# Expert outputs added into memory by adding scatters, in a one-core block of a long convolution and a mixture of experts

## The reference, cut to what matters

```
x1 = x + layernorm(s4d_block(layernorm(x)))
u  = layernorm(x1)                                # input of the expert layer, "normalised rows"
z  = layernorm(u) * g + b
w  = the two largest of softmax(z @ rW + rb), each over their sum     # 2 of 8 experts per token
mixed = sum over the two experts e of w[e] * (gelu(z @ W1[e] + b1[e]) @ W2[e] + b2[e])
out = x1 + layernorm(u + mixed)
```

## Time and profile before

| | |
|---|---|
| median of three runs | 616.25 us |
| the profiled execution | 617.41 us, of which the profile's span is 615.5 |
| PE busy | 516.5 us (84%) |
| DVE busy | 462.6 us (75%) |
| ACT busy | 347.2 us (56%) |
| POOL busy | 223.3 us (36%) |
| moved by DMA | 69.59 MB |

### The profile page before, as it was taken

One profiled execution on the slowest core, in us unless ns is written; L12 is line 12 of the kernel. 1 busy time (PEld: TensorE's weight loads), 2 busy tenths in 40 slices (PEclk: granted clock), 3 DMA queues, 4 the chain that ended last, 5 costly groups with the idle time before them and its releaser, 6 DMA issues. The chain is left out here.

```text
span 615.5 us, 12632 instructions
## 1 busy us (share of the span) xinstructions
PE 516.5 (84%) x2927; PEld 428.5 (70%) x2928; DVE 462.6 (75%) x1412; ACT 347.2 (56%) x751; POOL 223.3 (36%) x195
## 2 busy tenths in 40 slices
PE   0379899869979778978999999999999999957850
PEld 0139888759868664444798888888888988945640
DVE  6999787997886963873687787777778777732885
ACT  6982755654855568431555555555555555561584
POOL 0000666237676773662132232232322322332410
PEclk9997999989989979869999999999999999986995
DMA  6206600101111788245622222222222222119923
GB/s 162 114 0 246 233 1 1 69 2 70 43 53 43 275 269 285 98 142 134 184 79 70 68 86 68 68 86 68 68 77 77 69 78 76 60 43 366 351 103 136
DMA packets 37261, 69.59 MB, mean 113 GB/s; under 512 B 7568, under 2 KB 23696, under 8 KB 36720
## 3 DMA queue, kind: packets, MB, share of 16 engines
q1 hardware_dynamic: 30752, 51.48, 25.9%
q0 software_dynamic: 6480, 17.77, 8.1%
HBM read 42.02 MB, written 27.21 MB: 112 GB/s over the span
## 5 line engine op out<-in xcount | busy, mean ns | idle before, releaser
L1157 POOL DMA_INDIRECT y_rows<-y_sb,dst x71 | 74.7, 1052 | 195.9 <-DVE y_sb L1043 138.6
L1349 PE MATMUL psum<-ws,z_hl 128*128 x426 | 117.3, 410 | 2.0 <-DVE z_hl L1020 2.0
L1368 PE MATMUL psum<-ws,h_hl 128*128 x852 | 115.9, 285 | 0.1
L1368 PEld LDWEIGHTS psum<-ws,h_hl 128*128 128x128 f32 x852 | 103.5, 189 | 0.3 <-issue 0.3
L1121 POOL DMA_INDIRECT z_rows<-zn,pos x64 | 73.3, 1146 | 39.8 <-DVE pos L881 23.2
L1349 PEld LDWEIGHTS psum<-ws,z_hl 128*128 128x128 f32 x426 | 75.2, 188 | 17.1 <-issue 3.0
L595 ACT CAST h_hl<-psum 128x512 fp32r<-128x512 f32 x71 | 41.7, 587 | 72.5 <-PE psum L1358 72.4
L1028 DVE TENSOR_TENSOR hb<-psum,b1r 128x512 f32<-128x512 f32 x71 | 49.1, 692 | 35.3 <-issue 33.8
L587 ACT ACTIVATE z_f<-psum,gb 128x128 f32<-128x128 f32 x142 | 57.0, 452 | 16.7 <-PE psum L1336 14.7
L601 ACT ACTIVATE hg<-hb 128x512 f32<-128x512 f32 x71 | 44.9, 632 | 36.1 <-DVE hb L1028 35.8
L1224 PE MATMUL psum<-pm,ft 128*128 128x256 f32 x256 | 60.2, 395 | 0.4 <-DVE tmp L840 0.4
(11 more groups left out here) (207 smaller groups left out, 887.7 us busy)
## 6 DMA issues: line engine op xcount, KB each, us to landing
z_in<-z_rows SPq DMA_DIRECT2D x71, 129.0 KB
w_raw<-in_dram SPq DMA_DIRECT2D x16, 512.0 KB, 5.6
ya<-y_rows SPq DMA_DIRECT2D x16, 512.0 KB, 5.6
xs<-in_dram SPq DMA_DIRECT2D x8, 512.0 KB, 5.7
x_dram<-xs SPq DMA_DIRECT2D x8, 512.0 KB
out_dram<-acc SPq DMA_DIRECT2D x8, 512.0 KB, 2.6
b1r<-in_dram SPq DMA_DIRECT2D x8, 256.0 KB
x1m<-x_dram SPq DMA_DIRECT2D x4, 512.0 KB
```

The costliest lines, as they stand in the source:

```text
L1157: pool.indirect_dma_start(y_rows, bass.IndirectOffsetOnAxis(ap=dst[q][:, 0:1], axis=0), y_sb[q][:, :], None).then_inc(sem(f"y_out{q}"), 16)
L1349: last = TE.matmul(ps_h[q], z_hl[q][:, a, k], w_at(e1, c, k * F, F), start=n == 0, stop=n == 5)
L1368: last = TE.matmul(ps_y[q], h_hl[q][:, a, k], w_at(e2, c, 1024 + k * H, H), start=n == 0, stop=n == 11)
```

## The change

It replaces the two rows for each token in `y_rows` by one, and has the DMA add into it.

- Stage one: SP stores each batch's normalised rows `zn` to `y_rows` (`store_rows`), 8 stores of 512 KB, each behind the store of x1. These stores now stand ahead of expert 4's weights. ACT also waits for `zn_stored` before it overwrites a `zn` buffer. Two stores of 128 rows of filler set the 2 x 128 rows that padding goes to. The root and the two operations on `rsm` that served `base` are gone.
- Ahead of the loop: the weights `wgt` are stored to `w_rows`, and DVE makes a table `order` that says for each tile how far the scatters of the other parity must have landed: to the one two before the previous tile where the expert is the same, to the previous tile where it is not.
- Per tile: DVE writes `row_of` (the token), then `flag`, then `widx` (which weight). POOL gathers 128 weights of 4 bytes into `wt` by `widx`, four tiles ahead of the scatter. ACT multiplies `y_sb` by `wt` into `yw`, behind `hg` in its part. POOL scatters `yw` with addition into `y_rows`. It waits for SP's `released` and for the scatter two tiles before. SP issues a `release` for tile t behind the load of tile t+6.
- Tail: 8 loads `yr` of 512 KB instead of 16, and x1's load of 2 MB stands ahead of the third. No diagonal matrices, no matmul, no `base`, no sum. DVE takes statistics straight from `yr`, with the results in PSUM. POOL adds x1, except for the last half batch, which DVE adds. All is written out without hardware loops.

```diff
-TRASH = 2 * B * T
+TRASH = B * T
@@ SP, stage one
+            def store_rows(lo, hi):
+                for b in range(lo, hi):
+                    sp.wait_ge(sem("x1_ready"), b + 1)
+                    sp.dma_start(x1_dram[:, b], xs[b][:, :, :]).then_inc(sem("x1_stored"), 16)
+                    sp.wait_ge(sem("zn_ready"), b + 1)
+                    sp.dma_start(y_tok[:, b], zn[buf(b)][:, :, 0:H]).then_inc(sem(f"zn_stored{buf(b)}"), 16)
+                sp.wait_ge(sem("x1_stored"), 16 * hi)
+            store_rows(0, 4)
+            load_expert(sp, 5)
+            store_rows(4, 5)
             sp.wait_ge(sem("kf_mm"), 2)
             sp.wait_ge(sem("fwd_mm"), 16)
             load_expert(sp, 4)
...
@@ SP, tile loop
+            def release(t, q):
+                behind = sp.value_load(order[0:1, bass.ds(t, 1)], min_val=16, max_val=16 * TILES)
+                sp.wait_ge(sem(f"y_out{1 - q}"), behind)
+                sp.sem_inc(sem("released"), 1)
...
+            with sp.Fori(3, (TILES - 3) // 2) as j:
                 load_z(j * 2 + 2, 0)
+                release(j * 2 - 4, 0)
                 load_z(j * 2 + 3, 1)
+                release(j * 2 - 3, 1)
@@ SP, tail
             for n in range(B):
...
+                if n == 2:
+                    sp.wait_ge(sem("x1_in"), 64)
                     sp.dma_start(x1m[:, 0:4], x1_dram[:, 0:4]).then_inc(sem("x1_in"), 16)
+                sp.dma_start(yr[:, n], y_tok[:, B - 1 - n]).then_inc(sem(f"y_in{n}"), 16)
@@ ACT, part(i), behind hg
+                t, q = i - 2, par
+                if live(t):
+                    act.wait_ge(sem("y_ready"), t + 1)
+                    gate(act)
+                    act.wait_ge(sem(f"w_in{q}"), (t - q) * 8 + 16)
+                    m = slot(t, u, -2)
+                    if not early(t, 3):
+                        act.wait_ge(sem(f"y_out{1 - q}"), (t - 2 + q) * 8)
+                    nc.scalar.activation(yw[m % 3][:, :], y_sb[q][:, :], ACT.Identity, scale=wt[m][:, 0:1]).then_inc(sem("yw_ready"), 1)
@@ ACT, tail
+            def close(n):
+                act.wait_ge(sem("m_var"), n + 1)
+                nc.scalar.activation(rm[:, n % 2, 0, :], mvm[n % 2][:, :, 1], ACT.Sqrt, bias=eps[:, 0:1]).then_inc(sem("m_sd"), 1)
+                act.wait_ge(sem("m_rs"), n + 1)
                 for k in range(4):
+                    last = nc.scalar.activation(acc[:, n, k], yr[:, n, k], ACT.Identity,
+                                                bias=rm[:, n % 2, 2, k:k + 1], scale=rm[:, n % 2, 1, k:k + 1])
...
@@ DVE, part(i)
                     dve.wait_ge(sem(f"z_in{q}"), (t - q) * 8 + 16)
+                    if q:
+                        V.scalar_tensor_tensor(row_of[:, bass.ds(t, 1)], z_in[q][:, H + 1:W], 0.0, z_in[q][:, H:H + 1], ALU.min, ALU.add)
+                    else:
+                        V.tensor_copy(row_of[:, bass.ds(t, 1)], z_in[q][:, H:H + 1])
                     V.tensor_scalar(flag[:, :], ...
                     dve.wait_ge(sem("flag_set"), t + 1)
-                    V.tensor_tensor(dest[:, bass.ds(t, 1)], z_in[q][:, H:H + 1], flag[:, :],
+                    if not early(t, 3):
+                        dve.wait_ge(sem(f"w_in{1 - q}"), (t - 2 + q) * 8)
+                    gate(dve)
+                    V.tensor_tensor(widx[slot(t, u, 2) % 3][:, :], z_in[q][:, H:H + 1], flag[:, :],
                                     ALU.add).then_inc(sem("dest_ready"), 1)
...
-                        dve.wait_ge(sem(f"y_out{q}"), (t - q) * 8)
+                        dve.wait_ge(sem("yw_ready"), t - 1)
@@ DVE, tail
+            spread_of(0)                     # waits y_in, bn_stats x4, bn_aggr x4 into PSUM
+            for n in range(B):
+                if n + 1 < B:
+                    spread_of(n + 1)
+                scale(n)                     # waits m_sd, reciprocal, multiply, subtract
@@ POOL, tile loop and tail
+            with pool.Fori(1, (TILES - 5) // UNROLL) as j:
+                for u in range(UNROLL):
+                    gather_w(j * UNROLL + (5 + u), (1 + u) % 2, (5 + u) % 6)
+                    scatter_y(j * UNROLL + (1 + u), (1 + u) % 2, (1 + u) % 6)
...
+            def add(n, ks):
+                pool.wait_ge(sem("m_fin"), n + 1)
...
+                G.tensor_tensor(acc[:, n, ks], acc[:, n, ks], x1m[:, B - 1 - n, ks], ALU.add).then_inc(sem("m_out"), 1)
```

More of the change, by code:

```diff
@@ L149, in program @@
     tab_e = at("tab_e", [P, TILES + 1], F32, c0 + 5952)
-    dest = at("dest", [P, TILES + 1], U32, c0 + 6240)
-    dst = [at(f"dst{i}", [P, 1], U32, c0 + 6528 + 32 * i) for i in range(2)]
+    dst = [at(f"dst{i}", [P, 1], U32, o0 + 71 * KB + 256 + 32 * i) for i in range(6)]
+    row_of = at("row_of", [P, TILES + 1], U32, o0 + 71 * KB + 448)
+    order = at("order", [1, TILES + 1], I32, o0 + 71 * KB + 736)
+    widx = [at(f"widx{i}", [P, 1], U32, o0 + 71 * KB + 32 * i) for i in range(3)]
+    wt = [at(f"wt{i}", [P, 1], F32, o0 + 50 * KB + 768 + 32 * i) for i in range(6)]
+    yw = [at(f"yw{i}", [P, H], F32, o0 + k * KB) for i, k in enumerate((69, 70, 49))]
     flag = at("flag", [P, 1], F32, c0 + 6592)
@@ L204, in wide_bank @@
         return bank(2 + n % 6).rearrange("p (s h) -> p s h", s=2)
+    mvm = [bank(i)[:, 0:8].rearrange("p (k c) -> p k c", k=4) for i in range(2)]
+    m_shift = [bank(2 + i)[:, 0:4] for i in range(2)]
     def k_block(ht, j, to):
@@ L254, in program, with tiles @@
     loaded = {}
-    def tiles(eng, part):
+    def tiles(eng, part, peel=0):
         loaded[eng.engine.name] = {}
-        for i in range(-2, 3):
+        for i in range(-2, 3 + UNROLL * peel):
             part(i, i % 2, i)
-        with eng.Fori(0, (TILES - 5) // UNROLL) as j:
+        with eng.Fori(peel, (TILES - 5) // UNROLL) as j:
             loaded[eng.engine.name] = {}
@@ L277, in back @@
         return n * -1 + (B - 1)
-    ps_mix = [bank(2 * i, 2) for i in range(2)]
+    y_tok = y_rows[0:TRASH, :].rearrange("(p b k) h -> p b k h", b=B, k=4)
     def route(b):
@@ L572, in _ @@
             act.wait_ge(sem("pad_set"), 1)
-            nc.scalar.activation(rsm[:, 0], mv1[:, :, :, 1], ACT.Sqrt, bias=eps[:, 0:1], scale=1.0 / H).then_inc(sem("rsm_sd"), 1)
             act.wait_ge(sem("wsm_sub"), 1)
@@ L615, in close @@
-            def close(b, par):
-                act.wait_ge(sem("m_var"), b + 1)
-                nc.scalar.activation(rm[:, par, 0, :], mvm[par][:, :, 1], ACT.Sqrt, bias=eps[:, 0:1]).then_inc(sem("m_sd"), 1)
-                act.wait_ge(sem("m_rs"), b + 1)
-                for k in range(4):
-                    row = acc[:, bass.ds(b, 1), k].rearrange("p a h -> p (a h)")
-                    last = nc.scalar.activation(row, row, ACT.Identity,
-                                                bias=rm[:, par, 2, k:k + 1], scale=rm[:, par, 1, k:k + 1])
-                last.then_inc(sem("m_fin"), 1)
@@ L1076, in add @@
-            def add(n):
-                dve.wait_ge(sem("m_fin"), n + 1)
-                row = acc[:, bass.ds(n, 1)]
-                V.tensor_tensor(row, row, x1m[:, bass.ds(back(n), 1)], ALU.add).then_inc(sem("m_out"), 1)
-            mix(0, 0)
-            for n in range(3):
-                mix(n + 1, (n + 1) % 2)
-                scale(n, n % 2)
-                if n:
-                    add(n - 1)
-            dve.wait_ge(sem("x1_in"), 80)
-            with dve.Fori(1, B // 2 - 1) as j:
-                mix(j * 2 + 2, 0)
-                scale(j * 2 + 1, 1)
-                add(j * 2)
-                mix(j * 2 + 3, 1)
-                scale(j * 2 + 2, 0)
-                add(j * 2 + 1)
@@ L1099, in _ @@
+            spread_of(0)
+            for n in range(B):
+                if n + 1 < B:
+                    spread_of(n + 1)
+                scale(n)
+            dve.wait_ge(sem("m_fin"), B + 1)
+            dve.wait_ge(sem("x1_in"), 80)
+            V.tensor_tensor(acc[:, B - 1, 2:4], acc[:, B - 1, 2:4], x1m[:, 0, 2:4], ALU.add).then_inc(sem("m_last"), 1)
         @block.gpsimd
@@ L1176, in _, with gather_w @@
-            weights(0, 0)
-            weights(1, 1)
-            with pool.Fori(1, B // 2) as j:
-                weights(j * 2, 0)
-                weights(j * 2 + 1, 1)
+            def gather_w(t, q, m):
+                if not early(t, 2):
+                    pool.wait_ge(sem(f"w_in{q}"), (t - q) * 8)
+                    gate(pool)
+                pool.wait_ge(sem("dest_ready"), t + 1)
+                gate(pool)
+                pool.indirect_dma_start(wt[m][:, 0:1], None, w_rows,
+                                        bass.IndirectOffsetOnAxis(ap=widx[m % 3][:, 0:1], axis=0)).then_inc(sem(f"w_in{q}"), 16)
@@ L1182, in _ @@
+            for t in range(TILES - 4, TILES):
+                scatter_y(t, t % 2, t % 6)
+            def add(n, ks):
+                pool.wait_ge(sem("m_fin"), n + 1)
+                if n % 4 == 0:
+                    pool.wait_ge(sem("x1_in"), 80 if n else 64)
```

(3 more changed lines are left out.)

206 lines of the change are left out of this document (79 added, 127 removed).

## The result

The changed kernel took 609.05 us (median of four runs, 608.85 to 609.19), the one before beside it 616.45 (614.77 to 617.18). The ratio is 0.9883, with a 95% interval of 0.9863 to 0.9904: faster by 1.2%, where 616.5 and no change was forecast. The profiled execution took 609.15 us with a span of 607.3, against 617.41 and 615.5: 8.2 us less.

| stretch | before | after | difference | forecast |
|---|---|---|---|---|
| stage one, to the first `hb` | 294.16 | 294.24 | +0.1 | +0.5 |
| first `hb` to PE's last matmul | 252.3 | 266.2 | +13.9 | +23.6 |
| last matmul to the tail's first load | 6.8 | 8.2 | +1.4 | -2.0 |
| first load of the tail to the end | 62.2 | 38.7 | -23.5 | -22.8 |
| sum | | | -8.2 | -0.7 |

What follows compares the result with a forecast made beforehand. PE, DVE and a ring through DVE and ACT were all taken to bound the loop at 3.45 us a part. 617.4 + 23.6 (loop) - 2.0 (to tail) - 22.8 (tail) + 0.5 (stage one) = 616.7, given as 616.5; range 602 to 632.

Steps and rivals of the forecast that it cites:

- the ring has slack: Rival, tile loop: `z_f` held by PE, `yw` hides, only DVE's 0.2 per part felt; 606 us, faster; chance 0.24.
- What bounds the loop: Tile loop: PE, DVE and the ring `hb`, `hg`, `z_f`, `z_hl`, next `hb` through DVE and ACT, all at 3.45 us.
- DVE is the dearer one: Rival, tile loop: `row_of` 0.33, gate and wait 0.14 lengthen DVE's path in every part; 625 us, slower; chance 0.22.
- the adds don't flow: Rival, tile loop: scatter round trips over 7.5 us or POOL's pair over 3.85; 637 us and more; chance 0.08.
- The ordinary part: Four of six parts per loop round: `yw` 0.46 on the ring less 0.07 ACT slack, +0.39 us each.
- The long parts: Two parts per round, longer (3.83, 3.74) for second fetch and branch back: counted +0.2 and +0.25 us.
- The parts outside the loop: Eight parts outside the eleven rounds, some still bound by loads: +1.5 us.
- From the loop to the tail: PE's last matmul to the tail's first load: 4.8 us instead of 6.8, last two scatters overlapping; -2.0 us.
- The tail: From its first load, T, to the end: T+39.4 instead of T+62.2, ACT's chain 3.1 per batch; -22.8 us.
- Stage one: Before the tile loop: 4 MB more of stores beside work, +0.5 us, bounds -2 and +4.
- hole ahead of batch 1: Tail: batch 1 waits for the third load, behind x1's 2 MB, and its statistics; a hole of 4 us.

Runs made afterwards that it cites:

- one-operation kernels: Kernel before plus one unused 128x256 ACT operation per tile: between `hg` and `z_f` 633.38 us, ratio 1.0243; between `z_f` and the hidden values' high part 619.13, 1.0001.
- written out kernels: Tile loop written out without hardware loop for PE, ACT, DVE: kernel before 616.43 us, changed 604.73, changed with `yw` moved off the ring 596.25.
- moved kernel: Changed kernel with ACT's `yw` moved from behind `hg` to between `z_f` and the hidden values' high part: 609.89 us, ratio 0.982; again 613.69, 0.9942.

## Why the prediction was wrong, point by point

The forecast of 616.5 lies 7.5 us above the 609.05, inside the range of 602 to 632, but "no change" was wrong: the kernel is faster by 1.2%. By stretches the loop was priced 9.7 too dear, the tail 0.7 and stage one 0.4; the stretch from the loop to the tail was 3.4 too cheap and hid a part of it. The loop came out at the lower bound, +14, that the prediction gave for nothing in the long parts. The rival "the ring has slack" had 606, nearer in number than 616.5; its mechanism, `yw` hidden behind the matmuls, did not happen.

- **What bounds the loop: right.** Ring through DVE and ACT, `z_hl` now behind `z_f` with a wait for ACT, `yw` between `hg` and `z_f`, DVE's additions hidden. The rivals "the ring has slack", "DVE is the dearer one" and "the adds don't flow" fall with the waits and the one-operation kernels (the third for the loop; at the loop's end the adds do cost, see below).
- **The ordinary part: right in mechanism, sized 0.1 too high.** +0.39 forecast, part 3.84; measured +0.29 to +0.30, part 3.74 or 3.75. `yw` takes 0.40 on the ring, not 0.46, and `z_f` to `z_hl` fell from 0.92 to 0.81, so the slack was 0.11, not 0.07. It lies below even my lower bound of 0.42, which was read from an operation of stage one. The rule that I had weighed against the rows (the Trainium skill, "VectorE: DVE Perf Modes", section "The TRN2 errata") gives 0.40 us for 256 elements, and the trace agrees: `z_f` starts 0.40 behind `yw`. In the sum: 4 x 0.1 x 11 = 4.4 us of the 9.7 that the loop was off.
- **The long parts: wrong, the step that failed.** "In the two long parts DVE's path is longer than ACT's by the fetch and the branch, and I count 0.2 and 0.25": 11 x 0.45 = 5.0 us. Measured: 3.83 and 3.74 became 3.82 and 3.74, nothing. The branch's delay is not a length that adds to a part; it lies beside the ring, and a ring of 3.74 covers it but for 0.08, because PE makes up for its 1.04 us in the parts that follow. The one-operation kernel shows the same, the written out ones that the excess belongs to the branch. With nothing for the long parts the same sum gives 611.5, faster. That the branch is covered is not a law: with plain scatters the same ring had parts of 4.35 to 4.4 once a round.
- **The parts outside the loop: right**, 1.5 forecast, 1.3 measured.
- **From the loop to the tail: wrong in sign.** 4.8 us forecast, 8.2 measured; with plain scatters the changed kernel takes 4.9 and its last one lands in 2.40, so the difference is the addition's. I let the last two scatters overlap on POOL. But the last parts have no first layer and are under 2 us apart (558.87 and 560.63 for `dst`), and POOL needs 2.2 to 2.4 for each adding scatter: it falls behind, 2.6 us of the miss. The landing of 3.82 instead of 2.40, of which 0.5 was counted, is the rest. The rule on additions by DMA (the Trainium skill, "Collectives: The Full Stack", section "The bandwidth ceiling: the fold count and why AG ≠ RS ≠ AR", half the rate, stated there for a collective that adds) speaks in the right direction: at about the same GB/s the DMA share in the changed kernel's loop is 0.44 with the addition and 0.23 without it, a factor of 1.9. The round trip rose by a factor of 1.6.
- **The tail: right**, -22.8 and -23.5; hole ahead of batch 1 as told, batch 1 closed at T+16.4 (17.1 forecast), 2.87 per batch instead of 3.1, since the root lasts 0.16 there and 0.28 in the earlier trace rows. (ACT's four operations were put at 2.06; the row says 2.08.)
- **Stage one: right** within its bounds, +0.1 for +0.5.
- **The expectations that missed:** that moving `yw` would bring the ring's price back in full; that a plain scatter would give 605 us (616.72; the 9.9 us that this expectation names for the end of the loop were 8.2); that it is either the addition or the gathers that makes the pauses; that the written out kernels come to 3.74 and 3.45 to 3.55 per part (3.70 and 3.60); that second fetches would cost something or nothing in the moved kernel (they gained 9 us); and that the late load of x1 adds its 3 us to every kernel. Where the pauses come from is open. Shown: in the moved kernel they came every round only with the round's branch; both indirect DMAs have a part in them there (fewer without the addition, smaller without the gathers); they are no wait for a weight; and in the largest of them ACT and DVE wait for PE. Not shown: what makes PE's results late.

## What to carry to other kernels

An operation's price is set by its place on the ring of engines, not by the engine's idle share: the same 0.4 us a tile cost 15 us in one place of ACT's queue and nothing in another. When a period grows, what was irregular in it (a branch, a second fetch) is covered first; add the growth to the ordinary parts and only the excess over the new period to the long ones. Where a profile models the ends of matmuls, check a wait without a releaser against what the waiting engine waits for in the kernel's text. Behind a loop that drains faster than it runs, look at the engine that issues the DMAs: its time per issue becomes the bound there.

## What the runs showed of the hardware that I had not expected

- A scatter of 128 rows of 1 KB that adds keeps POOL for 1625 ns on average in the loop, a plain one 1045; it lands in 3.82 us instead of 2.40 at the loop's end. The mean busy share of the DMA engines in the loop is 0.44 with the addition and 0.23 without, at about 70 GB/s.
- A gather of 128 values of 4 bytes keeps POOL for 983 ns. With ACT neither using nor awaiting the values, the moved kernel took 614.4 us with the gathers and 601.8 without them and what belongs to them.
- A hardware loop's branch once per six parts cost 0.66 us of a round of 21.4 where nothing covered it, and 0.08 where the ring left PE 0.3 us a part to catch up.
- The waits of ACT for PE's transposes ended within 0.11 us of the modelled ends in every kernel whose parts stay at 4.5 us or less, and 0.7 to 3.98 us behind them at the worst in those that have longer ones.
- With more register fetches the moved kernel, written out, ran 9 us faster (587.1 against 596.25), repeated at 586.8; I have no cause for it.
